# A two-layer compressed interaction network on one core: the remainder is multiplied from the gathered rows and placed by DMAs, lookups read the row table itself, and the far cast moves ahead of x1rep's copy

## The reference, cut to what matters

```
e   = stack(tbl_f[ids[:, f]])                               # (b, 32, 64)
x1  = relu(einsum('bhd,bmd,ohm->bod', e, e, W1) + b1)       # (b, 128, 64)
x2  = relu(einsum('bhd,bmd,ohm->bod', x1[:, :64], e, W2) + b2)
z   = sum over d of concat(x1[:, 64:], x2)                  # (b, 192)
y   = relu(relu([z, dense_ctx] @ W_top1 + b) @ W_top2 + b) @ W_top3
```

## Time and profile before

| | us |
|---|---|
| runs before | 2031.25, 2034.03, 2035.14 (median 2034.03) |
| the profiled execution | 2035.26 |
| its span, first to last instruction | 2033.5 |
| PE busy | 1999.9 (98%) |
| DVE busy | 1923.5 (95%) |
| ACT busy | 1713.6 (84%) |
| POOL busy | 1647.3 (81%) |
| mean granted TensorE clock | 0.997 |

### The profile page before, as it was taken

The page is one execution under the profiler, slowest core; times in us unless marked ns, Lnnn a source line. Parts: engine busy times, 40 slices in busy tenths (PEclk is TensorE's granted clock), DMA queues, the critical chain, the costliest instruction groups (busy, mean ns, idle before and its releaser), DMA issues.

```text
span 2033.5 us, 24093 instructions
## 1 busy us (share of the span) xinstructions
PE 1999.9 (98%) x7038; PEld 1325.8 (65%) x7038; DVE 1923.5 (95%) x546; ACT 1713.6 (84%) x4887; POOL 1647.3 (81%) x708
## 2 busy tenths in 40 slices
PE   5999999999999999999999999999999999999999
PEld 3666666666666666666666666666666666666664
DVE  6999999999999999999999999999999999999991
ACT  4788888888888888888888888888888888888873
POOL 5898887879899998887889998788999988887520
PEclk9999999999999999999999999999999999999999
DMA  7898988988988989989989989989988989989950
GB/s 227 217 268 235 245 246 232 245 248 232 245 249 234 248 244 235 250 241 236 253 237 237 254 237 236 257 232 237 257 233 238 255 231 239 255 230 238 251 131 11
DMA packets 257782, 474.16 MB, mean 233 GB/s; under 512 B 35425, under 2 KB 52321, under 8 KB 257522
## 3 DMA queue, kind: packets, MB, share of 16 engines
q1 hardware_dynamic: 230450, 396.18, 64.5%
q0 software_dynamic: 26624, 75.52, 22.0%
q10 hardware_dynamic: 576, 0.92, 0.1%
HBM read 321.49 MB, written 16.78 MB: 166 GB/s over the span
## 4 chain that ended last, share of the span: by engine, by line
PE 90%; DMA 3%; DVE 2%; ACT 2%; issue 2%; POOL 1%; SPq 0%; DVEq 0%; POOLq 0%; ACTq 0%
PE acc L592 20%; PE acc L604 17%; PE acc L605 17%; PE acc L610 17%; PE acc L615 14%; DMA plo<-pnear 2%; DVE pnear L514 2%; PE acc L595 1%; ACT phi L789 1%; ACT x L713 1%; POOL prod L308 1%; DMA x1rep<-x 1%; PE x1p L686 0%; DMA near<-emb_rows 0%; PE acc L686 0%
## 5 line engine op out<-in xcount | busy, mean ns | idle before, releaser
L271 POOL DMA_INDIRECT gathered<-in_tables,idx x256 | 655.4, 2560 | 101.8 <-POOL idx L266 51.2
L308 POOL TENSOR_TENSOR prod<-near,h 128x2048 f32<-128x2048 f32 x126 | 582.5, 4623 | 128.5 <-PE acc L595 81.1
L604 PE MATMUL acc<-phi,w2lo 128*128 128x512 f32 x1664 | 655.2, 394 | 8.2 <-ACT phi L789 8.0
L605 PE MATMUL acc<-phi,w2hi 128*128 128x512 f32 x1664 | 654.3, 393 | 0.0
L514 DVE TENSOR_TENSOR pnear<-near,x1p 128x4096 f32<-128x4096 f32 x128 | 564.9, 4413 | 6.2 <-ACT x1p L762 3.8
L514 DVE TENSOR_TENSOR pfar<-far,x1p 128x4096 f32<-128x4096 f32 x128 | 564.9, 4413 | 0.7 <-PE acc L615 0.7
L592 PE MATMUL acc<-prod,w1T 128*128 128x512 f32 x1024 | 460.1, 592 | 1.5 <-DVE prod L489 1.5
L610 PE MATMUL acc<-plo,w2hi 128*128 128x512 f32 x1664 | 454.5, 423 | 0.0
L713 ACT ACTIVATE x<-acc,bias 128x64 f32<-128x64 f32 x1024 | 305.8, 324 | 170.6 <-PE acc L595 170.6
L519 DVE TENSOR_TENSOR plo<-pnear,phi 128x3072 fp32r<-128x3072 f32 x128 | 446.2, 3486 | 0.3 <-ACT phi L789 0.3
L519 DVE TENSOR_TENSOR plo<-pfar,phi 128x2560 fp32r<-128x2560 f32 x128 | 361.2, 2822 | 45.1 <-ACT phi L801 45.0
(11 more groups left out here) (75 smaller groups left out, 1151.3 us busy)
## 6 DMA issues: line engine op xcount, KB each, us to landing
far<-emb_rows SPq DMA_DIRECT2D x512, 256.0 KB, 4.6
near<-emb_rows SPq DMA_DIRECT2D x510, 256.0 KB
plo<-pnear POOLq DMA_DIRECT2D x128, 512.0 KB
x1rep<-x SPq DMA_DIRECT2D x255, 256.0 KB, 4.3
h<-emb_rows SPq DMA_DIRECT2D x128, 256.0 KB
emb_rows<-gathered SPq DMA_DIRECT2D x127, 128.0 KB
gathered<-in_tables,idx POOLq DMA_INDIRECT x256, 6.6
rem_a<-emb_rows SPq DMA_DIRECT2D x64, 64.0 KB
```

Source lines behind the costliest of these rows:

```text
L271: nc.gpsimd.indirect_dma_start(out=gathered[s][:, g, :], out_offset=None, in_=a["tables"], in_offset=bass.IndirectOffsetOnAxis(ap=idx[s][: ...
L308: nc.gpsimd.tensor_tensor(prod1[:, :, :], near[(u + 2) % 3][:, :, :], h0[odd][:, :].unsqueeze(1).to_broadcast([P, K1, N]), ALU.mult).then_ ...
L604: nc.tensor.matmul(acc2[s][:, :], w2lo[:, t, :], phi[:, t, :], start=(t == T_DMA), stop=False)
L605: mm = nc.tensor.matmul(acc2[s][:, :], w2hi[:, t, :], phi[:, t, :], start=False, stop=(t == T_SPLIT - 1))
```

## The change

1. `rem_a` goes. `rem_b` (64 partitions of 256 numbers) is now filled by one DMA from the upper 64 partitions of `gathered` (`move_upper`), and POOL multiplies it with the lower 64 partitions. ACT casts the product once into `rem_hi`, POOL subtracts into `rem_lo`, and SP writes three DMAs of 64 KB (`place_remainder`: the high part twice, the low part once) into `rem_parts`, of which there are now two. PE waits for these DMAs (`rem_in`).
2. `place_idx` and `idx` go; the indirect DMA takes its offsets from `idx_all`.
3. ACT casts the far tiles (line 801) right after the near ones, then copies `x1rep`, then casts the DMA's two tiles (line 790), then casts the remainder.
4. PE multiplies the DMA's two tiles after `layer1` instead of ahead of it.
5. In the prologue, POOL does the first remainders, after all twelve first lookups, instead of DVE; and ACT casts the first of them ahead of its staging of `w2`.

```diff
 gpsimd:
-                    in_offset=bass.IndirectOffsetOnAxis(ap=idx[s][:, g:g + 1], axis=0)).then_inc(rows_gathered[s], 16)
+                    in_offset=bass.IndirectOffsetOnAxis(ap=idx_all[:, g, pair:pair + 1], axis=0)).then_inc(rows_gathered[s], 16)
+            def remainder_products(pair, s):
+                pool.wait_ge(rem_b_in, 16 * pair + 16)
+                if pair:
+                    pool.wait_ge(rem_lo_ready, pair)
+                nc.gpsimd.tensor_tensor(rem_prod[:, :], gathered[s][0:HALF * GS, :, :].rearrange("p g d -> p (g d)"),
+                                        rem_b[:, :, :].rearrange("p g d -> p (g d)"), ALU.mult).then_inc(rem_prod_ready, 1)
...
             def step(c, turn, u, at):
+                if not odd and begun(at) and within(at, 2):
+                    remainder_low(pair + 1)
...
                 if odd and within(at, 3):
-                    remainder_products(pair + 2)
+                    remainder_products(pair + 2, (u // 2 + 2) % 3)
...
-            remainder_products(1)
+            for pair in range(2):
+                remainder_products(pair, pair)
+                remainder_low(pair)
 sync:
+            def move_upper(pair, s):
+                if pair:
+                    sp.wait_ge(rem_prod_ready, pair)
+                sp.dma_start(rem_b[:, :, :], gathered[s][HALF * GS:F * GS, :, :]).then_inc(rem_b_in, 16)
+
+            def place_remainder(pair):
+                sp.wait_ge(rem_lo_ready, pair + 1)
+                if pair >= 2:
+                    sp.wait_ge(acc1_ready, 2 * pair - 2)
+                for b, part in enumerate((rem_hi, rem_hi, rem_lo)):
+                    home = rem_parts[pair % 2][b * REM:(b + 1) * REM, :].rearrange("r (w n) -> r w n", w=2)
+                    sp.dma_start(home.bitcast(fp32), part[:, :].bitcast(fp32)).then_inc(rem_in, 16)
...
+                    if odd:
+                        sp.wait_ge(emb_stored, STORES * (pair + 3))
                     load_near(sp, (c + 3) * N, 1 - odd, u % 3)
+                if not odd and begun(at) and within(at, 2):
+                    place_remainder(pair + 1)
                 if not odd and within(at, 5):
                     store_rows(pair + 2, (u // 2 + 2) % 3, turn + (u // 2 + 2) // 3 + 1)
+                    move_upper(pair + 2, (u // 2 + 2) % 3)
                 if within(at, 2):
                     sp.wait_ge(pfar_ready, c + 1)
                     load_far((c + 2) * N, odd)
-                if not odd and within(at, 5):
-                    sp.wait_ge(emb_stored, STORES * pair + 3 * STORES)
-                    sp.sem_inc(stores_begun, 1)
-                    sp.wait_ge(rem_prod_ready, pair + 2)
-                    load_rem((c + 4) * N)
 tensor:
                 high(odd, range(T_DMA, T_NEAR))
-                pe.wait_ge(hi_dma_ready, c + 1)
-                high(odd, range(0, T_DMA)).then_inc(hi_near_used, 1)
                 if within(at, 2):
                     pe.wait_ge(p1_ready, c + 3)
-                    pe.wait_ge(rem_lo_ready, pair + 2)
+                    pe.wait_ge(rem_in, 48 * (pair + 2))
                     pe.wait_ge(z1_ready, c + 1)
-                    layer1(odd)
+                    layer1(odd, pair + 1)
...
+                pe.wait_ge(hi_dma_ready, c + 1)
+                high(odd, range(0, T_DMA)).then_inc(hi_near_used, 1)
                 pe.wait_ge(pfar_ready, c + 1)
 scalar:
-                nc.scalar.copy(phi[:, 0:T_DMA, :], products[:, 0:T_DMA, :]).then_inc(hi_dma_ready, 1)
+                act.wait_ge(pfar_ready, c + 1)
+                if begun(at):
+                    act.wait_ge(acc2_ready, c)
+                nc.scalar.copy(phi[:, T_NEAR:T_SPLIT, :], pfar[...][:, 0:T_SPLIT - T_NEAR, :]).then_inc(hi_far_ready, 1)
                 if within(at, 1):
...
                     copy_x1rep(1 - odd)
+                nc.scalar.copy(phi[:, 0:T_DMA, :], products[:, 0:T_DMA, :]).then_inc(hi_dma_ready, 1)
+                if odd and within(at, 3):
+                    remainder_hi(pair + 2)
```

More of the change, by code:

```diff
@@ L66, in build_dlrm @@
         idx_all = sb("idx_all", [P, PAIR_GATHERS, PAIRS], i32)
-        idx = [sb(f"idx_{s}", [P, PAIR_GATHERS], i32) for s in range(3)]
         gathered = [sb(f"gathered_{s}", [P, PAIR_GATHERS, D]) for s in range(3)]
@@ L82, in build_dlrm @@
         far = [sb(f"far_{s}", [P, K2, N]) for s in range(2)]
[L83 to L86, removed]
+        rem_b = sb("rem_b", [HALF * GS, PAIR_GATHERS, D])
+        rem_prod = sb("rem_prod", [HALF * GS, PAIR_GATHERS * D])
+        rem_hi = sb("rem_hi", [HALF * GS, PAIR_GATHERS * D], fp32r)
+        rem_lo = sb("rem_lo", [HALF * GS, PAIR_GATHERS * D], fp32r)
+        rem_parts = [sb(f"rem_parts_{s}", [3 * REM, N], fp32r) for s in range(2)]
         prod1 = sb("prod1", [P, K1, N])
@@ L152, in build_dlrm @@
         x1p_ready = sem("x1p_ready")
+        rem_b_in = sem("rem_b_in")
         rem_in = sem("rem_in")
@@ L263, in _, with gather @@
             pool.wait_ge(idx_all_ready, 1)
[L265 to L270, removed]
+            def gather(g, pair, s):
                 nc.gpsimd.indirect_dma_start(
                     out=gathered[s][:, g, :], out_offset=None, in_=a["tables"],
-                    in_offset=bass.IndirectOffsetOnAxis(ap=idx[s][:, g:g + 1], axis=0)).then_inc(rows_gathered[s], 16)
[L275 to L279, removed]
+                    in_offset=bass.IndirectOffsetOnAxis(ap=idx_all[:, g, pair:pair + 1], axis=0)).then_inc(rows_gathered[s], 16)
[5 more added lines that the diff above has]
+                                        rem_b[:, :, :].rearrange("p g d -> p (g d)"), ALU.mult).then_inc(rem_prod_ready, 1)
             def low_parts(c):
@@ L288, in _ @@
             for pair in range(3):
-                place_idx(pair, pair)
                 for g in range(PAIR_GATHERS):
-                    gather(g, pair)
+                    gather(g, pair, pair)
+                pool.sem_inc(lookups_begun, 1)
             def remainder_low(pair):
                 pool.wait_ge(rem_hi_ready, pair + 1)
-                nc.gpsimd.tensor_tensor(rem_parts[2 * REM:3 * REM, :], rem_prod[:, :],
-                                        rem_parts[0:REM, :].bitcast(fp32), ALU.subtract).then_inc(rem_lo_ready, 1)
+                nc.gpsimd.tensor_tensor(rem_lo[:, :], rem_prod[:, :], rem_hi[:, :].bitcast(fp32),
+                                        ALU.subtract).then_inc(rem_lo_ready, 1)
             def step(c, turn, u, at):
                 pair, odd = turn * (U // 2) + u // 2, u % 2
[L300 to L303, removed]
+                if not odd and begun(at) and within(at, 2):
+                    remainder_low(pair + 1)
                 if within(at, 2):
@@ L324, in step @@
                         pool.wait_ge(emb_stored, STORES * pair + STORES)
-                        place_idx(pair + 3, u // 2)
+                        pool.wait_ge(rem_prod_ready, pair + 1)
                     for g in range(2 * odd, 2 * odd + 2):
-                        gather(g, u // 2)
-            remainder_products(1)
+                        gather(g, pair + 3, u // 2)
+            for pair in range(2):
+                remainder_products(pair, pair)
+                remainder_low(pair)
             all_steps(step)
@@ L362, in _ @@
             store_copy(sp, 0, 0, 0)
+            move_upper(0, 0)
             sp.wait_ge(emb_stored, STORES)
@@ L365, in _ @@
             load_near_tiles(sp, 0, 0, range(0, K1 // 2))
-            load_rem(0)
             load_near(sp, N, 1, 1)
             store_rows(1, 1, 1)
+            move_upper(1, 1)
+            place_remainder(0)
             load_far(0, 0)
             sp.wait_ge(emb_stored, 2 * STORES)
-            sp.wait_ge(rem_prod_ready, 1)
-            load_rem(2 * N)
             sp.wait_ge(z1_ready, 1)
             replicate_x1(sp, [0])
+            place_remainder(1)
             sp.wait_ge(tp_copied, 2)
@@ L495, in _ @@
             products1(0, slice(K1 // 2, K1)).then_inc(p1_ready, 1)
-            dve.wait_ge(rem_in, 32)
-            nc.vector.tensor_tensor(rem_prod[:, :], rem_a[:, :], rem_b[:, :], ALU.mult).then_inc(rem_prod_ready, 1)
             dve.wait_ge(tp_filled, 5)
@@ L526, in step @@
                     dve.wait_ge(lo_near_ready, c)
+                    dve.wait_ge(hi_dma_ready, c)
                     dve.wait_ge(lo_dma_in, 16 * c)
@@ L592, in tiles1, with remainder1, layer1 @@
                     nc.tensor.matmul(acc1[s][:, :], w1T[:, k, :], prod1[:, k, :], start=(k == 0), stop=False)
-            def remainder1(s):
-                nc.tensor.matmul(acc1[s][:, :], w1remT[:, s, :], rem_parts[:, :],
+            def remainder1(s, pair):
+                nc.tensor.matmul(acc1[s][:, :], w1remT[:, s, :], rem_parts[pair % 2][:, :],
                                  start=False, stop=True).then_inc(acc1_ready, 1)
-            def layer1(s):
+            def layer1(s, pair):
                 tiles1(s, range(K1))
-                remainder1(s)
```

(22 more changed lines are left out.)

10 lines of the change are left out of this document (1 added, 9 removed).

## The result

The changed kernel took 2482.9 us (median of four runs, 2479.8 to 2488.0) against 2034.3 us before: a ratio of 1.221, 95% interval 1.219 to 1.224. I had forecast 2400 us, from 2190 to 2475. The sign and the place were right, the time lies 8 us above the range.

A forecast was written before the change was run, and what follows sets the result against it. PE's own work was taken as the bound. 62 even steps of 3.7 us stall plus 2.2 us low clock add 366 us; with -3 for the new orders and +3 for the prologue, 2400 us, range 2190 to 2475.

The forecast's parts named there:

- The new wait: Ahead of layer1 in 62 even steps, PE waits for the placement DMAs behind SP's list; 3.7 us idle each.
- the signs that I named: Profile after: 62 PE waits of 3 to 4.5 us, some 230 us; PE busy below 90%; clock half in a tenth.
- the stall's size: Idle time per even step: placement lands at 15.9 us, PE asks at 12.2, so 3.7 us; ends 1.8 and 4.4.
- the two deductions: Taken off the stores' 16.4 us landing: 0.2 us for smaller size, 0.3 us for emptier queues with longer pairs.
- The upper end of my range for the landing: Slowest of four store landings in the kernel before: 16.6 us after the remainder matmul, a 4.4 us stall.
- The low clock: PE at half clock after each even-step stall: 2.2 us lost each, ends 0 and 2.7.
- Prologue: Start of the kernel: first remainder follows twelve lookups and delays ACT's staging and PE's first layer1; +3 us, ends 0 and +6.
- the step that I had named: Prologue: ACT waits for POOL's first remainder ahead of its staging, which ends near 26.3 us instead of 20.0.
- the direct lookups as a gain: Prologue: without three index copies and their waits, about 1 us each, the lookups end at 23.8 us instead of 26.8.
- PE's order: DMA's two tiles behind layer1 on PE: changes nothing, since they leave one stretch and enter the other.
- The new orders' gain: ACT's early far cast frees DVE's 45.0 us of waits and some PE idle time; -3 us, ends -12 and 0.
- Rival 3: Faster: placement lands within 12.2 us, PE never waits, DVE's freed time cuts idle time; 2025 us at best, chance 0.04.

The follow-up runs named there:

- e1: Changed kernel with PE's wait for the placed remainder moved behind the eight layer 1 tile records, just before the remainder's matmul: 2197 us, 1.079 times before.
- e3: Changed kernel with the placement issued later in SP's list, behind the stores, the upper rows' move and the far loads: 2784 us, 1.367 times before.
- e5: Changed kernel with the placement issued at the head of the even step, ahead of x1rep: 2034.8 us, 1.0002 times before.
- e13: Changed kernel with ACT's order of before and even steps' lookups held back until the placement has landed: 2478 us, 1.218 times before.
- e4: Changed kernel with five extra matmuls on PE ahead of the placement wait in the 62 even steps: 2385 us, 1.171 times before.
- e2: Changed kernel with the placement issued right behind x1rep, ahead of h0 and near: 2138 us, 1.050 times before.
- e9: Changed kernel where, in even steps, POOL waits for the placement before issuing its two lookups: 2477 us, 1.218 times before.
- e10: Changed kernel where, in even steps, POOL waits for the placement before issuing the plo DMA and the lookups: 2489 us, 1.224 times before.
- e6: As e5, with ACT's cast of the first remainder put back behind its staging of w2: 2031.9 us, 0.9985 times before.
- e11: Kernel before with the direct lookups alone, without index copies: 2038.5 us, 1.0018 times before.
- e14: Changed kernel with PE's order of before, the DMA's two tiles ahead of layer1: 2591 us, 1.273 times before.
- e12: Kernel before with only ACT's and PE's new order (far cast early, DMA's tiles cast last and multiplied behind layer1): 2027.8 us, 0.997 times before.

## Why the prediction was right and where it failed

**The new wait: right.** Place, count (62), the chain through SP's list and its restart at each odd chunk's L596 are what the profile shows; e1 shortens the wait by moving its end, e3 lengthens it and e5 removes it by moving the issue. Of the signs that I named, PE's wait was 321 us in all instead of 230, and its share of busy time fell to 86%.

**The step that failed is the stall's size, "I take 0.2 us off for the smaller size and 0.3 because with longer pairs less is left in the queues", 15.9 us.** The placement landed at 17.4 us, so PE idled 5.18 us and not 3.7: 62 x 1.48 = 92 us. The stores' 16.4 us from the earlier trace rows was the right row (16.5 as a mean in the trace before); no row stood behind the two deductions, and both were wrong. `near` alone landed at 16.7 us, 0.9 later than before. Longer pairs took nothing off it: in e5, whose steps are 15.2 us again, it landed at 16.6. Of the 0.9 us, the lookups beside it, which no longer had an index copy ahead of them, and ACT's later sums are 0.5 us together (e13: 16.2). The placement stood 0.7 us behind `near`, as the stores had (0.8), though smaller. What the last 0.4 us of `near` are stays open. The upper end of my range for the landing, 16.6 us, came from four landings of the stores in the kernel before and was too low for the same reason. I also wrote that SP had issued 1.5 MB just before; with `x1rep` it is 1.75 MB.

**The low clock: right.** 2.2 us forecast; an even step took 22.44 us, and 22.44 - 15.20 - 5.18 = 2.06 us. e4 gives 1.6 of it back. The Trainium skill's rule (TensorE: Matmul & The Clock Gate, HAM oscillation), that the transition is paid at each wait, agrees with the trace: mean clock 0.926, and a granted clock of 0.50 for a time after each of the 62 waits. After the 1.4 us of idle time of e2 (mean clock 0.996) there was next to none.

**A DMA lands by what is beside it.** The Trainium skill (DMA: Bandwidth & Descriptors, Queues, rings and completion order) says that each DMA engine takes turns between the queues that have work for it, packet by packet. e9 and e10 agree in so far as the other queue's work counts: plo's DMA and the lookups are in POOL's queue, not in SP's, and with both held back the placement landed 2.3 us sooner, with the lookups alone 0.4. That the turns go packet by packet no run here shows.

**The other parts.** Prologue: +3 forecast, the remainder matmul's first start moved from 28.9 to 33.1 us, +4.2; e6 took 2.9 us back by the step that I had named. But I had counted the direct lookups as a gain there, and alone they cost as much (e11). PE's order "changes nothing": wrong with ACT's order (e14), since I looked at PE's list alone. The new orders' gain, 3 us, was 7 us where PE is not held up (e12); under the stall its part at the end stays, 69.8 us behind the last remainder matmul's start instead of 73.4. Rival 3, faster, fell. Its condition, a landing before PE asks, holds in e5 and e6, and they lie at or 3 us under the kernel before.

**The sum.** 62 x (5.18 + 2.06) = 449 us against 366, and 2483 against 2400 us: 83 us of error, the stall's 92 less the clock's 62 x 0.14 = 9. Prologue (+4.2) and end (-3.5) nearly cancel.

## What to carry to other kernels

When a transfer is moved into an engine's DMA list, find what is issued ahead of it in the same step, and what released that: here three copies of 64 KB stood behind 1.75 MB that started only after the previous result of the very engine that waited for it. Place it where the queue is idle, before the bulk loads and not after them, and ask for it just before its use. Judge the DMA engines in the stretch of the wait, and not by their mean: here 0.98 against 0.76. Price such a landing from the nearest transfer in the same place of the queue and deduct nothing without a row.

## What the runs showed of the hardware that I had not expected

- A shorter wait need not be a shorter step: landings of 17.4, 17.1 and 16.8 us (changed kernel, e9, e13) all gave even steps of 22.3 to 22.4 us, the difference went into the low clock (mean 0.926, 0.917, 0.915).
- Three DMAs of 64 KB with 7 us of lead and only `x1rep` ahead in their queue still landed 5.6 us after the last was issued (e2). Issued into an idle queue (e5) they landed 3.4 us after it.
- POOL busy 1403.5 us instead of 1647.3 was worth nothing, and the direct lookups alone (e11, POOL 1584.9) cost 0.2%, in the prologue.
